# The order of a DLRM tower's two steps: four gram halves in two pairs at the head of each step, the MLP stages behind them

## The reference

```
e = stack([tbl_f[ids[:, f]] for f in range(26)], axis=1)            # 2048 x 26 x 128
combined = concatenate([dense[:, None, :], e], axis=1)              # 2048 x 27 x 128
inter = einsum('bnd,bmd->bnm', combined, combined)                  # 2048 x 27 x 27
z = concatenate([dense, inter[:, triu_i, triu_j]], axis=1)
h = concatenate([z, dense], axis=1)                                 # 2048 x 607
h = maximum(h @ W_top1 + b_top1, 0)                                 # 512
h = maximum(h @ W_top2 + b_top2, 0)                                 # 256
y = h @ W_top3                                                      # 1
```

## Time and profile before

| | before |
|---|---|
| median of the three executions shown, us | 602.82 |
| time of the profiled execution, us | 605.72 |
| span of the profiled execution (first to last instruction), us | 603.9 |
| PE busy, us (share) | 433.2 (72%) |
| weight loads busy, us (share) | 389.7 (65%) |
| DVE busy, us (share) | 263.3 (44%) |
| POOL busy, us (share) | 253.8 (42%) |
| ACT busy, us (share) | 207.4 (34%) |
| mean granted clock of TensorE | 0.822 |

### The profile page before, as it was taken

The page is one execution under the profiler, slowest core; times in us unless marked ns, Lnnn a source line. Parts: engine busy times, 40 slices in busy tenths (PEclk is TensorE's granted clock), DMA queues, the critical chain, the costliest instruction groups (busy, mean ns, idle before and its releaser), DMA issues.

```text
span 603.9 us, 13994 instructions
## 1 busy us (share of the span) xinstructions
PE 433.2 (72%) x6369; PEld 389.7 (65%) x6369; DVE 263.3 (44%) x258; ACT 207.4 (34%) x313; POOL 253.8 (42%) x261
## 2 busy tenths in 40 slices
PE   3773277766788677787778778786777867787927
PEld 3672157655767667676667767675676766777827
DVE  5981035671544424535244434554154442465221
ACT  3550023443313333234222433233332333335713
POOL 7787545374423445154351644345433344500000
PEclk9886557987868788888787888896887878889978
DMA  8923113031102111031110311121111211101010
GB/s 202 243 55 104 39 32 99 21 108 37 27 25 83 45 33 41 18 92 33 27 45 16 101 34 27 37 86 47 29 26 29 85 42 33 41 7 58 4 58 1
DMA packets 21909, 32.79 MB, mean 54 GB/s; under 512 B 8030, under 2 KB 14846, under 8 KB 21850
## 3 DMA queue, kind: packets, MB, share of 16 engines
q0 software_dynamic: 8288, 16.83, 11.0%
q1 hardware_dynamic: 13562, 15.06, 8.8%
HBM read 28.24 MB, written 3.68 MB: 53 GB/s over the span
## 4 chain that ended last, share of the span: by engine, by line
PE 56%; issue 16%; DVE 12%; ACT 9%; another core or an unknown queue 6%; DMA 1%; SPq 0%; DVEq 0%
PE hot_ps L617 23%; PE gram_ps L642 11%; DVE one_hot L503 9%; PE mlp_ps L649 6%; PE transpose_ps L593 5%; PE mlp_ps L650 5%; PE mlp_ps L651 5%; ACT embed_t L424 4%; ACT embed_t L379 3%; PE hot_ids_ps L599 2%; DVE packed_lo L507 1%; DVE units L489 1%; DMA bounce<-units 1%; DMA rows<-bounce 1%
## 5 line engine op out<-in xcount | busy, mean ns | idle before, releaser
L351 POOL DMA_INDIRECT rows<-table,ids_sb x256 | 252.9, 988 | 272.9 <-PE transpose_ps L593 199.4
L617 PE MATMUL hot_ps<-one_hot,table_hi 125*128 125x256 f32 x640 | 200.2, 338 | 65.7 <-ACT embed_t L424 43.6
L503 DVE TENSOR_TENSOR one_hot<-hot_ids_ps,row_numbers_sb 125x1024 fp32r<-125x1024 f32 x160 | 192.4, 1236 | 110.9 <-PE hot_ids_ps L599 59.4
L617 PEld LDWEIGHTS hot_ps<-one_hot,table_hi 125*128 125x128 f32 x640 | 142.2, 222 | 81.3 <-DVE one_hot L503 46.0
L617 PE MATMUL hot_ps<-one_hot,table_lo 125*128 125x256 f32 x640 | 185.4, 315 | 0.0
L617 PEld LDWEIGHTS hot_ps<-one_hot,table_lo 125*128 125x128 f32 x640 | 143.5, 224 | 0.0
L642 PE MATMUL gram_ps<-embed_t 128*27 128x27 f32 x4096 | 77.3, 205 | 67.0 <-issue 66.1
L642 PEld LDWEIGHTS gram_ps<-embed_t 128*27 128x27 f32 x4096 | 58.8, 117 | 88.2 <-issue 85.3
L379 ACT COPY embed_t<-transpose_ps 128x512 f32<-128x512 f32 (+1 forms) x80 | 85.3, 1066 | 79.9 <-PE transpose_ps L593 51.1
L424 ACT COPY embed_t<-hot_ps 128x256 f32<-128x256 f32 x80 | 54.8, 684 | 148.2 <-PE hot_ps L617 82.1
L489 DVE COPY_PREDICATED units<-late_sb,gram_ps 128x208 f32<-128x208 int32 x32 | 35.1, 1098 | 121.2 <-ACT units L418 115.3
(11 more groups left out here) (49 smaller groups left out, 314.6 us busy)
## 6 DMA issues: line engine op xcount, KB each, us to landing
rows<-table,ids_sb POOLq DMA_INDIRECT x256
embed_t<-table SPq DMA_DIRECT2D x8, 448.0 KB
bounce<-units SPq DMA_DIRECT2D x8, 448.0 KB
scratch<-bounce SPq DMA_DIRECT2D x7, 378.0 KB
rows<-dense SPq DMA_DIRECT2D x16, 64.0 KB
scratch<-table SPq DMA_DIRECT2D x2, 448.0 KB
scratch<-w SPq DMA_DIRECT2D x1, 512.0 KB
scratch<-w_units SPq DMA_DIRECT2D x2, 252.0 KB
```

The costliest lines, as they stand in the source:

```text
L351: nc.gpsimd.indirect_dma_start(rows[:, t2, f, :], None, tables[table], bass.IndirectOffsetOnAxis(ids_sb[:, slot, table:table + 1], 0)).the ...
L503: nc.vector.tensor_tensor(one_hot[:, n % RING], ids_over, numbers_over, ALU.is_equal).then_inc(one_hot_ready, 1)
L617: last = nc.tensor.matmul(hot_ps[:, 0:GROUP], table[:, k % HOT, step, :], one_hot[:, (2 * k + half) % RING, j, :], start=(step == 0 and ta ...
```

## The change

Only the lists of step names change; no instruction is added or removed. In both steps G0 and G1 stand together at the head, then one look-up half and Q0, then G2 and G3; the MLP stages and the remaining look-ups follow.

```diff
 STEPS = [
-    "D0 S0 M0 G0 Q0 G1 M1 G2 Q1 W0 M2 G3 H0 M3 H1 Q2 H2 W1 H3 Q3 H4 H5 W2 Q4 H6 H7".split(),
-    "G0 H8 G1 H9 Q0 H10 G2 H11 M4 G3 H12 Q1 H13 W3 M5 H14 Q2 H15 W4 M6 H16 Q3 H17 W5 Q4 H18 H19".split(),
+    "D0 S0 G0 G1 H0 Q0 G2 G3 M0 H1 Q1 M1 H2 W0 M2 H3 M3 Q2 H4 W1 H5 Q3 H6 W2 Q4 H7".split(),
+    "G0 G1 H8 Q0 G2 G3 M4 H9 H10 Q1 M5 H11 H12 Q2 M6 H13 H14 W3 H15 Q3 H16 W4 H17 H18 W5 Q4 H19".split(),
 ]
 
 LAST_STEPS = [
-    "D0 S0 M0 G0 Q0 G1 M1 G2 Q1 M2 G3 M3 Q2 M4 M5 Q3 M6 Q4".split(),
+    "D0 S0 G0 G1 Q0 M0 G2 G3 M1 Q1 M2 M3 Q2 M4 M5 Q3 M6 Q4".split(),
     "G0 G1 G2 G3".split(),
 ]
```

## The result

The changed kernel takes **618.76 us** (median of 4 runs, 617.16 to 623.08); the kernel before, beside it, 602.94 (4 runs, 600.51 to 607.83). The ratio is 1.0263, 95% interval 1.0179 to 1.0348: slower, by 16 us, where 572 us (550 to 603) was forecast. That it is slower is clear of the noise; whether by 2% or more is not. Disturbed runs are left out of this ratio and of all that follow, which is why a ratio need not be that of the medians beside it.

A forecast was written before the change was run, and what follows sets the result against it. PE's stream was taken to set the time, with 16% of the chain "issue", laid to gathers. Terms summed to -5.2 us a steady group, -31 in all: 605.7 to 574.6, less 2.9 to the median: 572 us (550 to 603).

The forecast's parts named there:

- the first term: G2 and G3 of the first step and G2 of the second finish before gathers starve them: -8.6 us a group.
- The rule of rows 3: A gram half under gather transfers costs 2.6 to 3.0 us more than one outside them.
- The second step's head: G0 and G1 of the second step come sooner, into the gather burst: +1.5 us a group, 0 to 4.0.
- The rival: Both steps' G0 and G1 fall into gather bursts, four halves starved: +5.0 us a group, about 630 us; chance 0.08.
- The first step's head: G0 of the first step can meet the tail of Q4's gather: +1.0 us a group, 0 to 5.9.
- Bare look-up copies: Look-up halves newly back to back, or with only Q3 between, wait for copies: +2 us a group, 1 to 3.
- The group's head: G0, now ahead of M0, starts earlier than M0 did, waiting only for H19's copy: -1.1 us a group.
- Gathers over look-ups and MLP: Q0's and Q1's gathers newly fall on look-ups and MLP stages: +4 us a group, 3.5 to 4.9.
- clock: PE's low granted clock behind starved halves and idle, on M0, M2, M3, H11, M4, mostly goes: -4 us a group.
- the loss stays with the gathers: Rival: a gather costs PE the same whatever lies under it; +0.9 us a group, about 604 us; chance 0.18.
- The refill of instructions: Counter-evidence: if refill is mostly hidden, gram order matters little, the -8.6 is near 0, about +3 us a group.

The follow-up runs named there:

- e5: Changed kernel, from tile 2 on each gather brings 64 B of each row instead of 512, same number of GpSimd instructions: 629.6 us, 1.030 of the kernel before.
- e6: Changed kernel, from tile 2 on each gather replaced by a plain SyncE load of the same 64 KB: 459.9 us, 0.7525 of the kernel before.
- e3: Changed kernel with Q0 moved behind G3 in both steps (group 7's list stays): 566.2 us, 0.9422 of the kernel before.
- e9: Changed kernel, matmul order untouched; GpSimd waits for the step's G3 before its first bank's gathers: 570.5 us, 0.9509 of the kernel before.
- e14: Kernel before with only the second step's list changed, GpSimd's first-bank gathers waiting for G3: 1.0555 of the kernel before, on a 432 us chip.
- e13: Kernel before, order untouched, GpSimd's first-bank gathers waiting for G3: 0.9997 of the kernel before, which takes 432.1 us on that chip.
- e15: Kernel before with only the first step's list changed, GpSimd's first-bank gathers waiting for G3: 0.9367 of the kernel before, on a 432 us chip.
- e16: Changed kernel as it is, timed again on a chip where the kernel before takes 431.4 us: 439.1 us, 1.016 of it.
- e11: Changed kernel with Q0 behind G3 in the first step, and halves alternating with look-ups in the second: 566.9 us, 0.9376 of the kernel before.
- e12: Changed kernel with Q0 behind G3 in the first step, and M4 H8 M5 H9 ahead of the second's halves: 565.1 us, 0.9331 of before.
- e4: Changed kernel with all four gram halves heading each step and the five Q stages spread early behind them: 608.0 us, 1.0125 of the kernel before.
- e1: Kernel before without the gathers of tiles 2 to 15, rows in place used again: 453.0 us, beside 601.5 for the kernel before.
- e2: Changed kernel without the gathers of tiles 2 to 15, rows in place used again: 449.9 us, beside 601.5 for the kernel before.
- e18: Kernel before with only the first step's list changed, GpSimd's first-bank gathers waiting for G3, timed on a second 432 us chip: 0.9358 of before.

## Why the prediction was wrong

**The step that failed** is the first term, "G2 and G3 start 0.6 us behind the start of Q0 ... so both are done at about 1.9 us, ahead of the 2.9 us. Gone are ... -8.6". The start of the shortage was read from a G2 that had a slow stretch of look-ups ahead of it: 43 matmuls on time, 1.5 us behind the first gather. Behind a G2 at full pace there were none: the first pause comes 0.2 us behind the issue, 2.0 us after the start of Q0 in group 4, in place of the 2.9. G2 also starts 0.8 to 1.0 us behind Q0, not 0.6. Measured in groups 1 to 5: first step's G2 2.45 to 0.74, its G3 4.69 to 4.08, second step's G2 3.64 to 0.59, its G3 0.82 to 4.72 us. Sum -1.5, not -8.6. The rule of rows 3 ("a gram half under gather transfers") was also off: transfers are not it (e5, e6, and a first pause ahead of the first packet), the issuing is, and it bites some 1.3 us sooner. The group's sum came out at +0.6 in place of -5.2, and this term alone accounts for 7.1 us, more than the whole difference. e3 and e9 show that this step is where it turned: with G3 kept away from the issue the time is 566 and 570 us, beside the 572 that was forecast, though not by its terms.

That a full store of some 43 matmuls carried the old G2 over the first gather fits all of this, but it was only argued; no run measured the store.

**The second step's head**, +1.5 (0 to 4.0): near its size by its own reckoning, but not where it was put. From Q2 to the end of G1 a group took 17.5 us and takes 14.8; without H2 and H3 (2.1) and H8 with its broadcast (1.6) the old stretch is 13.8 us, so the cost is +1.0. But the two halves were to take 3 to 5 us together and take 8.5, G0 from 2.89 to 7.63 and G1 from 0.76 to 0.91, while Q4 and the look-ups ahead of them got shorter. A half is not starved for a set 2.94 us, it is starved until the burst ends, and all that the burst has left falls on whatever stands first. The rival named this place, and put "four halves" and 630 us to it; one half did it alone.

**The first step's head**, +1.0: measured -0.7; G0 and G1 were clear of Q4's gather.

**Bare look-up copies**, +2: undersized. Free of the toll, H8 to H19 take 3.7 us more with the second list (e14 against e13): 0.9 each at H9 and H11, 1.0 at H13, and 1.0 at H17, which the prediction did not list (before it, Q4 stood between H17 and H18). One of them in the changed kernel, ahead of H10 in group 4, is as the prediction said it would be, by ACT's copy:

```profile
406.80 0.36 PE L617 MATMUL hot_ps<-one_hot,table_hi 125*128 125x256 f32 x1 [0.85 <-ACT embed_t L424]
```

**The group's head**, -1.1, was right in sign and undersized: free of the toll H19 falls from 3.38 to 2.00 us and M0 from 2.78 to 1.52 (e13, e15), -2.6. In the changed kernel itself M0 falls by 0.7 us and H19 only from 3.52 to 3.42: the head's wait moved ahead of G0 and stayed. Fewer waits at Q2 and Q4 of the first step, -1.6 in the same pair of runs, was not in the sum at all.

**Gathers over look-ups and MLP**, +4, and **clock**, -4. M2 and M3 are at 1.47 and 1.42 us, the 1.5 that was forecast, and MLP stages fell by 5.6 a group. But M0, behind a starved G3, fell only to 2.32, and the mean granted clock of the whole run is 0.817, not above that of before. Look-ups rose by 7.1, of which e16 against e13 puts 2.7 to the order; the other 4.4 is toll, close to what was priced.

**The rivals.** The first, "the loss stays with the gathers" (0.18, 604 us), is the nearest: the toll per group is 23.5 before and 23.8 after, and the change as a whole, +0.6 a group in the table, is close to its +0.9. Its reason against, that halves lose two to three times as much per us as look-ups do (2.6 to 3.0 within 3.5, beside 0.28 to 0.39), is what misled: it is true of a place and not of the sum, since look-ups lose theirs as late copies (H13 alone takes 5.3 us in the changed kernel, 2.0 in e16). Its 604 us falls short of the 618.8 by what lies outside the steady groups, above all the +6.9 up to the start of group 1, 5.0 of them ahead of group 0's first half, in code that the change left alone.

**The refill of instructions.** The Trainium skill (Runtime: NRT & Kernel Launch, Instruction fetch mechanics) calls the refill of instructions mostly hidden. On the last two chips the trace agrees in the main: the halves pause for over 1 us four times in e16 and once in e13. Where the change was timed first the gram line idles 112.0 us, and the queue's row is the same, 50 packets and 0.82 MB, in all of them. That the missing supply beside the gathers is this refill is not shown, and the trace speaks against it: each of the pauses in e13 and e16 ends 2.3 to 2.7 us behind the start of a packet of that queue, while those in the changed kernel's steady groups lie anywhere from 0.8 to 17 us behind one.

**What stays open:** what differs between the chips, or between the times of the runs. The software queue's 8288 packets have a median of 0.06 us and the instruction queue's 50 packets one of 1.0 to 1.1 us on both kinds, and POOL's gather takes 0.97 to 0.99 us on both. Nothing in these rows tells which chip a trace is from, but PE does. Also open is why the toll's sum hardly moves with four orders, drops by 9 us in e3, e9, e11 and e12, and does not in e4.

## What to carry to other kernels

Where the gathers take their toll, a dense row of small matmuls right behind the stage that releases them is starved from GpSimd's first issue on; let the gathers wait for the row (one semaphore wait on GpSimd) or put the releasing stage behind it. Before pricing a move out of a slow place, ask who pays next: sum the places of all kinds of steps over a group, since a toll that leaves the matmuls can come back as a late copy on another engine. And count a pair of look-ups with nothing between them at 0.9 to 1.0 us each (H9, H11, H13 and H17 in e14), for every pair of the list.

## What was not expected of the hardware

- 224 indirect transfers issued by GpSimd cost about 150 us of 602 on one chip (e1), the kernel took 601 to 613 us in all the first sets of runs (three chips at least), and on two others, later, the same kernel takes 432 us. A verdict on an order holds for where it was taken; here the change is slower on both (1.026 and 1.016), the first list alone is faster on both (0.971, and 0.936 with the hold), and the hold takes the changed kernel from 1.026 to 0.951 of before where the toll exists and is worth, for the order of before, nothing where it does not.
- The same 64 KB tiles issued by SyncE cost next to nothing: 459.9 us (e6) beside 449.9 without any (e2, the same order, on another chip), and 48.8 us a group in both.
- Beside the issuing, TensorE passes about 5 gram matmuls each 0.72 to 0.75 us, with 27 columns or 9, and with rows of 512 B or 64 B.
- With GpSimd idle, a row of halves still has one pause of about 2 us now and then. PE's timeline of e4, with no gather issued near it:

```profile
358.80 0.64 PE L642 MATMUL gram_ps<-embed_t 128*27 128x27 f32 x52 [1.80 <-issue]
```

A packet of 16 KB on the instruction queue had begun 2.7 us earlier and took 1.3 us. The trace has more such cases: from group 0's second step on, e4's halves pause 14 times for over 1.5 us, and each pause ends 2.2 to 3.1 us behind the start of such a packet, as do all 22 pauses of over 1 us in the halves of e1, e2, e6 and e13 to e18. That the packet is the cause was not tried.
